# Taking x times Ws in plain fp32 on two halves of the array's columns, without splitting x

## The reference

```python
    def _L0_cond_ref(x, conv_w, conv_b, Wp, bp, Ws, bs, A_log, dt_log, Wo, bo):
        ...
        conv = conv_b + sum((x_pad[:, k:k + L, :] * conv_w[k, 0] for k in range(K)))
        proj = conv @ Wp + bp
        B_t = jax.nn.softplus(proj[..., :N])
        C_t = jnp.tanh(proj[..., N:])
        u = x @ Ws + bs
        ...
        def step(state, inputs):
            u_t, b_t, c_t = inputs
            state = decay * state + dt * b_t * u_t
            return (state, c_t * state)
        ...
        return y @ Wo + bo

    def _L1_cond_ref(x, h0, Wx, Wh, b):
        ...
        xW = jnp.einsum('ntd,dh->tnh', x, Wx) + b
        def step(h, xw_t):
            h_next = jnp.tanh(h @ Wh + xw_t)
            return (h_next, h_next)
        ...
    x = x + _L0_cond_ref(x, cond_1024[:, None, :], ...)
    x = x + _L1_cond_ref(x, cond_1024, L1_cond_Wx, L1_cond_Wh, L1_cond_b)
```

## Time and profile before

| | |
|---|---|
| median of 3 runs | 1162.56 us (1162.14 to 1163.04) |
| the profiled execution | 1162.89 us, span 1161.1 us |
| PE busy | 1153.1 us, 99% of the span |
| PE weight loads | 963.1 us, 83% |
| DVE, ACT, POOL busy | 697.5, 577.9, 356.1 us |
| granted clock of PE | 1.00 over the span |

### The profile page before, as it was taken

One profiled execution on the slowest core, in us unless ns is written; L12 is line 12 of the kernel. 1 busy time (PEld: TensorE's weight loads), 2 busy tenths in 40 slices (PEclk: granted clock), 3 DMA queues, 4 the chain that ended last, 5 costly groups with the idle time before them and its releaser, 6 DMA issues.

```text
span 1161.1 us, 16194 instructions
## 1 busy us (share of the span) xinstructions
PE 1153.1 (99%) x6000; PEld 963.1 (83%) x6000; DVE 697.5 (60%) x1103; ACT 577.9 (50%) x856; POOL 356.1 (31%) x202
## 2 busy tenths in 40 slices
PE   8999999999999999999999999999999999999998
PEld 8998999966888888888888888888888888888886
DVE  8767776675555655655565555555556556555553
ACT  7755665574535454545454545535454545453431
POOL 6200014023333333333333333333333333333330
PEclk9999999999999999999999999999999999999999
DMA  9797776602122222222222222222222222222202
GB/s 369 268 337 250 258 254 239 215 1 82 36 92 86 79 72 72 72 72 72 72 72 72 72 72 72 80 95 81 96 79 74 72 72 72 72 72 73 73 37 73
DMA packets 71762, 130.12 MB, mean 112 GB/s; under 512 B 3696, under 2 KB 29296, under 8 KB 71728
## 3 DMA queue, kind: packets, MB, share of 16 engines
q1 hardware_dynamic: 71728, 129.65, 33.2%
HBM read 96.08 MB, written 33.55 MB: 112 GB/s over the span
## 4 chain that ended last, share of the span: by engine, by line
PE 97%; DVE 1%; DMA 1%; ACT 0%; POOL 0%; issue 0%; SPq 0%; POOLq 0%; DVEq 0%; ACTq 0%
PE bank L926 10%; PE bank L934 10%; PE bank L935 10%; PE bank L920 10%; PE bank L938 10%; PE bank L919 10%; PE bank L835 10%; PE bank L981 5%; PE bank L852 5%; PE bank L895 3%; PE bank L901 3%; PE bank L909 2%; PE bank L910 2%; PE bank L870 2%; PE bank L867 2%; PE bank L868 2%
## 5 line engine op out<-in xcount | busy, mean ns | idle before, releaser
L451 POOL TENSOR_TENSOR x_lo<-x_f,x_hi 128x512 fp32r<-128x512 f32 x128 | 161.7, 1293 | 588.3 <-ACT x_hi L548 588.3
L580 ACT ACTIVATE h_f<-z_f 128x512 f32<-128x512 f32 x127 | 80.3, 632 | 291.3 <-DVE z_f L773 291.3
L934 PE MATMUL bank<-wh_hi,hT_hi 128*128 128x512 f32 x512 | 200.8, 392 | 0.0
L935 PE MATMUL bank<-wh_lo,hT_hi 128*128 128x512 f32 x512 | 199.9, 390 | 0.0
L920 PE MATMUL bank<-wx_lo,x_hi 128*128 128x512 f32 x512 | 199.7, 390 | 0.0
L919 PE MATMUL bank<-wx_hi,x_hi 128*128 128x512 f32 x512 | 199.6, 390 | 0.0
L782 DVE TENSOR_TENSOR hT_lo<-bank,hT_hi 128x512 fp32r<-128x512 f32 x127 | 88.0, 693 | 184.7 <-ACT hT_hi L584 184.7
L773 DVE TENSOR_TENSOR z_f<-bank,b_rows 128x512 f32<-128x512 f32 x127 | 87.9, 692 | 128.7 <-PE bank L938 125.7
L445 POOL TENSOR_TENSOR x_lo<-x_f,x_hi 128x2048 fp32r<-128x2048 f32 x32 | 147.7, 4616 | 1.5 <-PE bank L835 1.4
L926 PE MATMUL bank<-wx_hi,x_lo 128*128 128x512 f32 x512 | 144.8, 404 | 0.4 <-POOL x_lo L451 0.4
L938 PE MATMUL bank<-wh_hi,hT_lo 128*128 128x512 f32 x512 | 137.1, 389 | 0.0
(11 more groups left out here) (96 smaller groups left out, 1683.6 us busy)
## 6 DMA issues: line engine op xcount, KB each, us to landing
x_f<-x_dtb SPq DMA_DIRECT2D x32, 1024.0 KB, 8.0
out<-x_f SPq DMA_DIRECT2D x31, 1024.0 KB, 5.2
ring<-x_rev SPq DMA_DIRECT2D x55, 512.0 KB, 5.0
ring<-hankel SPq DMA_DIRECT2D x44, 512.0 KB, 4.0
x_early<-x_rev SPq DMA_DIRECT2D x8, 512.0 KB, 9.4
t_low<-low_rows SPq DMA_DIRECT2D x5, 512.0 KB, 7.7
wx_f<-Wx SPq DMA_DIRECT2D x1, 1024.0 KB, 7.9
wh_f<-Wh SPq DMA_DIRECT2D x1, 1024.0 KB, 7.7
```

The costliest lines, as they stand in the source:

```text
L451: nc.gpsimd.tensor_tensor(x1_lo[:, c], x1_f[par][:, c], f(x1_hi[:, c]), ALU.subtract)\
L580: nc.scalar.activation(h_f[:], z_f[:], ACT.Tanh).then_inc(h_ready, 1)
L934: nc.tensor.matmul(z, hT_hi[:, k], wh_hi[:, k], start=False, stop=False)
L935: nc.tensor.matmul(z, hT_hi[:, k], wh_lo[:, k], start=False, stop=False)
```

## The change

u of a group is now four plain fp32 matmuls straight from the loaded x, one for each 128 rows of D. Ws is no longer split, so each has 64 columns of weights. Even k write PSUM rows 0 to 63, and odd k rows 64 to 127; these are the two halves of the array's columns. As before the two halves of the bank are summed by ACT and DVE. All four matmuls stand in s = 0 (`u_product(g + 1)`). `split_x` on ACT, `split_x` and `x_rest` on POOL, the split of Ws and their buffers and semaphores go.

```diff
-        ws_hl = sb(ctx, "ws_hl", [P, KC, 2 * N], F32R)
+        ws_f = sb(ctx, "ws_f", [P, KC, N])
...
-            def split_x(g, par):
-                act.wait_ge(x_loaded[par], DMA * ((g - par) // 2 + 1) if isinstance(g, int) else (g - par) * (DMA // 2) + DMA)
-                wait(act, u_done, g)
-                nc.scalar.copy(x_hi[:], x_f[par][:]).then_inc(xhi_ready, 1)
...
                 for g, par in ((2 * pair + 1, 1), (2 * pair + 2, 0)):
                     x1_rest(g, par)
-                    x_rest(g + 1, 1 - par)
...
-            def u_first(g):
-
-                pe.wait_ge(xhi_ready, g + 1)
-                wait(pe, x1_ready, KC * g)
-                for k in range(KC):
-                    nc.tensor.matmul(UB[:], ws_hl[:, k], x_hi[:, k], start=(k == 0), stop=False)
-
-            def u_second(g):
-
-                pe.wait_ge(xlo_ready, g + 1)
-                for k in range(KC):
-                    mm = nc.tensor.matmul(UB[:], ws_hl[:, k], x_lo[:, k], start=False, stop=(k == KC - 1))
-                mm.then_inc(u_done, 1)
+            def u_product(g, par, some=range(KC)):
+
+                if 0 in some:
+                    pe.wait_ge(x_loaded[par], DMA * ((g - par) // 2 + 1) if isinstance(g, int) else (g - par) * (DMA // 2) + DMA)
+                    wait(pe, x1_ready, KC * g)
+                for k in some:
+                    rows = slice(k % 2 * N, k % 2 * N + N)
+                    mm = nc.tensor.matmul(UB[rows, :], ws_f[:, k], x_f[par][:, k].rearrange("p t b -> p (t b)"),
+                                          start=(k < 2), stop=(k >= KC - 2))
+                if KC - 1 in some:
+                    mm.then_inc(u_done, 1)
...
                 if m == 8:
-                    pe.wait_ge(weights_ready, 2)
-                    u_first(0)
-                    u_second(0)
+                    u_product(0, 0)
...
                     if s == 0 and not last:
-                        if first and par == 0:
-                            u_first(1)
-                        u_second(g + 1)
-                    if s == 3 and not (isinstance(g, int) and g == GROUPS - 2):
-                        u_first(g + 2)
+                        u_product(g + 1, 1 - par)
```

More of the change, by code:

```diff
@@ L102, in build @@
             wo_f = sb(unsplit, "wo_f", [P, D])
-            ws_f = sb(unsplit, "ws_f", [P, KC, N])
         wx_lo = sb(ctx, "wx_lo", [P, KC, D], F32R)
@@ L246, in build @@
         x_loaded = [sem(f"x_loaded{i}") for i in range(2)]
-        xhi_ready = sem("xhi_ready")
-        xlo_ready = sem("xlo_ready")
         u_done = sem("u_done")
@@ L412, in _ @@
             pool.wait_ge(ws_wo_loaded, 2 * DMA)
-            nc.gpsimd.tensor_copy(ws_hl[:, :, 0:N], ws_f[:]).then_inc(pool_step, 1)
+            pool.wait_ge(wo_scaled, 2)
+            nc.gpsimd.tensor_copy(wo_hi[:], wo_f[:]).then_inc(pool_step, 1)
             pool.wait_ge(pool_step, 1)
[L415 to L421, removed]
             nc.gpsimd.tensor_tensor(wo_lo[:], wo_f[:], f(wo_hi[:]), ALU.subtract).then_inc(weights_ready, 1)
@@ L425, in _ @@
             nc.gpsimd.tensor_copy(wx_hi[:], wx_f[:]).then_inc(pool_step, 1)
-            pool.wait_ge(pool_step, 3)
+            pool.wait_ge(pool_step, 2)
             nc.gpsimd.tensor_tensor(wx_lo[:], wx_f[:], f(wx_hi[:]), ALU.subtract).then_inc(weights_ready, 1)
@@ L429, in _ @@
             nc.gpsimd.tensor_copy(wh_hi[:], wh_f[:]).then_inc(pool_step, 1)
-            pool.wait_ge(pool_step, 4)
+            pool.wait_ge(pool_step, 3)
             nc.gpsimd.tensor_tensor(wh_lo[:], wh_f[:], f(wh_hi[:]), ALU.subtract).then_inc(weights_ready, 1)
@@ L452, in x1_rest @@
                       .then_inc(x1lo_ready, 1)
-            pool.wait_ge(conv_done, BANKS * KC - 2)
-            split_x(0, 0)
             pool.wait_ge(conv_done, BANKS * KC)
-            x_rest(0, 0)
             x1_rest(0, 0)
-            split_x(1, 1)
-            x_rest(1, 1)
             with pool.Fori(0, GROUPS // 2 - 1) as pair:
@@ L598, in steps @@
                         x1_copy(g + 1, 1 - par)
-                    if s == 1 and not (isinstance(g, int) and g == GROUPS - 2):
-                        split_x(g + 2, par)
             groups(act, steps)
@@ L950, in _ @@
                 if m == 18:
+                    pe.wait_ge(weights_ready, 1)
                     wo_product(0, FIRST_XB, range(0, 2))
@@ L955, in _ @@
                 if m == BANKS:
-                    pe.wait_ge(weights_ready, 4)
+                    pe.wait_ge(weights_ready, 3)
                     pe.wait_ge(turn_copied, BANKS * KC)
```

## The result

The change makes the kernel slower: 1190.58 us, median of 4 runs (1190.45 to 1191.03), against 1162.8 us for the kernel before on the same chip (4 runs). The ratio is 1.024 [1.0228, 1.0253]. The profiled execution took 1190.45 us, with a span of 1188.7 us, 27.6 us longer than that of before.

A forecast was written before the change was run, and what follows sets the result against it. PE's issue queue was taken to bound the kernel: 43.4 us for first steps, -0.9 for group 0, -7.2 for last steps and +0.5 ahead of the loop gave +35.8 us, so 1199 us. The range was 1180 to 1245 us.

The forecast's parts named there:

- The bound: Whole span: PE busy 99%, span a sum of its issue times; ACT and POOL edits count only where PE waits.
- The last steps: Step s = 3, groups 0 to 29: without u_first PE waits for x1_lo; 6.66 and 6.56 us, gain 7.2 us.
- The rival that the wait doesn't come: Last steps: x1_lo early enough to gain the whole 0.91 us each; 1179 us, chance within the rest's 0.02.
- The time of a record: New u matmuls: each is two records of 0.43 us, read from plain fp32 matmuls with 128 columns of weights.
- the rival of half-length records: u matmuls: 64-column records take 0.215 us; 1157 us with full overlap or 1164 us with five slots; chance 0.06.
- U: First step (s = 0): time of the four plain fp32 u matmuls, 2.31 us, records 2.15 plus switch 0.16.
- five slots: u matmuls: program order lets halves overlap only at three changes of half; 5 x 0.43 = 2.15 us, chance 0.42.
- The estimate from the same page's speedup of three tiles: u matmuls: at the skill page's share of ideal, two tiles give 1.59, so 3.44 / 1.59 = 2.16 us.
- The switch: u matmuls: going from whole array to halves and back costs 0 to 0.32 us; the middle, 0.16 us, taken.
- The sum: Whole kernel: +43.4 first steps, -0.9 group 0, -7.2 last steps, +0.5 ahead of the loop; together +35.8 us.
- the likeliest case: Whole kernel: u records take five slots; 1199 us, or 1194 to 1204 by the switch; chance 0.42.
- the full overlap: u matmuls, rival: the two halves overlap fully; +22.1 us, 1185 us (1180 without the switch), chance 0.15.

The follow-up runs named there:

- move_only: Kernel before, fp32r and split of x kept, with only the u_first matmuls moved from a group's last step to its first; 1182.38 us, 1.0172.
- move_dve_chunk: Kernel before with u_first moved to the first step and the last x1_lo chunk made by DVE instead of POOL; 1163.52 us, 1.0006.
- one_half: Changed kernel with all four u matmuls in PSUM rows 0 to 63, the upper half's products left out; 1244.94 us, 1.0709.
- u_twice: Changed kernel with the four u matmuls of a first step issued twice, same result; 1243.43 us, 1.0696.
- order_aabb: Changed kernel with u matmuls in order k = 0, 2, 1, 3, both of one half ahead of both of the other; 1190.79 us, 1.0243.
- full_width: Changed kernel with 128 columns of weights (Ws and 64 columns of zeros) in each u matmul, array never split; 1234.01 us, 1.0615.
- all_last: Changed kernel with all four u matmuls in the last step, for g + 2, and none in the first; 1184.74 us, 1.0192.

## Why the prediction was right or wrong, point by point

**The bound: right.** The work on PE and what PE waits for set the span. ACT and POOL lost 54.5 and 151.5 us (57 and 150 forecast), and nothing of it reached the span.

**The last steps: right.** Forecast were 6.56 to 6.66 us and -7.2 us in all, read from the one step of group 30. Measured are 6.62 us in the step shown and 203.82 / 31 = 6.57 in the mean, 31 waits of 12.0 us in total (0.39 each, 0.36 forecast), and -8.0 us. move_only and move_dve_chunk show the cause apart from the new matmuls. The rival that the wait doesn't come is refuted.

**The time of a record: right.** 0.43 us for 64 columns of weights, measured by one_half; the rival of half-length records, the only one that ended faster, falls.

**U: the step that failed.** The prediction said that "overlap comes only at the three places where the half changes, which leaves five slots", from the rule that records start in the order of the list. There are four: u_twice measures 1.70 us for the four matmuls without a switch, where the prediction had 2.15, and order_aabb shows why. A second record of A holds up only what follows on half A, and the other half goes on with its own. Every row of the kernel before used all columns, so their order said nothing of records on separate halves.

The Trainium skill, "TensorE: Matmul & The Clock Gate" (Part 3, what overlaps and what doesn't), states that matmuls start and end strictly in program order. By that order_aabb would have started its first pair only when half A was through with three of its four records; the trace shows a pair at the very start, so here the measurement decides against the rule as far as the starts go; the ends were not compared. The estimate from the same page's speedup of three tiles, U = 2.16 us, holds nothing for the switch. It came near 2.06 because the overlap it lacks (2.16 against 1.70 to 1.72 us of records) is about as large as the switch that it leaves out.

**The switch: mis-sized.** 0.16 us was taken, with bounds of 0 and 0.32; it is 0.34 us (one_half against full_width), just above the upper bound. The bounds came from how long a record outlasts its slot, which no run ties to this price.

The Trainium skill, "TensorEngine Tiling" (Tiling Modes, key properties), states that a change of the tiling mode drains the engine. The 0.34 us are in agreement with it, and so is u_twice, which stays on the halves and pays once; that the price is a drain, no run shows by itself.

**The sum.** In place of 2.31 us, U is 1.72 + 0.34 = 2.06: 0.25 us less in 31 first steps and once ahead of the loop, 8.0 us. The last steps give 0.8 us more. 35.8 - 8.0 - 0.8 = 27.0 us, measured 27.6. The time is 8.4 us from the forecast and below the likeliest case's own 1194 to 1204. It is in the range because the range, 65 us wide, took in the full overlap, the rival with a chance of 0.15. That rival had the right mechanism; its 1185 us was 5.6 us low, and 31 x (0.34 - 0.16) = 5.6 us is what its switch lacked. The two errors of U have opposite signs: the switch hid 0.18 us of the slot of 0.43 that was counted too much. That the forecast came as near as it did is in part luck.

## What to carry to other kernels

Work that stands ahead of a wait costs its own time and covers a part of the wait, and moving it elsewhere takes the cover away. Before moving it, look for a step of the same trace where it is absent (here the last step of group 30) and read what is left there. A move can also uncover a chain on another engine at the place it leaves, as all_last did on DVE. And an order that a trace shows is only shown for operations that share a resource; two matmuls on separate columns needed an experiment, and a list in the order A, A, B, B with one half alone beside it was enough to settle it.

## What the runs showed of the hardware

- Two plain fp32 matmuls with 64 columns of weights on different halves of the columns, with all 128 rows each, run side by side in full, in both orders of the list that were run (A, B, A, B and A, A, B, B): eight records in 1.70 us (u_twice) against 8 x 0.43 us on one half.
- Going from all columns to a half and back costs 0.34 us (one_half against full_width). Here 64 columns of weights and a half always go together, so the runs can't tell the one from the other. No row of the profile is the switch, but it shows in PE's starts: from the last transpose to the first u record 0.20 us in one_half against 0.11 in full_width, from there to the second record 0.48 against 0.43, and from the last u record to the second matmul of L891 0.86 against 0.67 (L892 there). PE's weight loads, first of the changed kernel and then of full_width:

```profile
631.26 0.20 PEld L864 LDWEIGHTS bank<-x_f,ws_f 128*64 128x64 f32 x4 [0.17 <-issue]
...
633.12 0.77 PEld L891 LDWEIGHTS bank<-wx_hi,x_lo 128*128 128x128 f32 x4 [0.81 <-issue]
```

```profile
648.41 0.30 PEld L865 LDWEIGHTS bank<-x_f,ws_f 128*128 128x128 f32 x2
...
651.53 0.19 PEld L892 LDWEIGHTS bank<-wx_hi,x_lo 128*128 128x128 f32 x1 [0.24 <-issue]
```

In full_width the first weight load of u starts 0.11 us ahead of its matmul (648.52), and the first one behind u starts at 651.53, together with the last u record. In the changed kernel both start only with their own matmuls (631.26 and 633.13), after 0.17 and 0.81 us without a load. So at both ends of the halves no weights are loaded ahead; whether the late load is the cause of the 0.34 us or goes along with it wasn't tried.

- Left open is u of several groups between one switch and the way back; no run here has it. By the figures above, as an estimate, four slots are 1.72 us of PE against 1.82, and each further group saves one switch of 0.34 us.
